# First routing of a mixture-of-experts kernel: the slots of the first two pairs of tiles ahead of their dense expert work

## What is computed

```python
x = x + 0.5 * ffn(layernorm(x), ...)
x = x + attention(layernorm(x), ...)
x = x + 0.5 * ffn(layernorm(x), ...)

def ffn(x, ...):
    scores = sigmoid(x @ gate_weight.T)              # 32 experts in 8 groups
    sfc = scores + bias
    # the 4 groups with the largest maximum, in them the 6 largest experts
    # combine weights: scores of the six, normalized, times 2.5
    for each expert: acc += c[:, None] * (silu(x @ gate.T) * (x @ up.T) @ down.T)
    shared = (silu(x @ shared_gate.T) * (x @ shared_up.T)) @ shared_down.T
    return acc + shared
```

## Time and profile before

| | us |
|---|---|
| median of three runs | 1548.52 |
| lowest and highest of the three | 1545.78 and 1552.76 |
| the profiled execution | 1545.28 |
| its span in the profile | 1543.5 |
| PE busy in the span | 1330.7 |
| POOL busy in the span | 924.0 |
| DVE busy in the span | 1067.6 |

### The profile page before, as it was taken

The page is one execution under the profiler, slowest core; times in us unless marked ns, Lnnn a source line. Parts: engine busy times, 40 slices in busy tenths (PEclk is TensorE's granted clock), DMA queues, the critical chain, the costliest instruction groups (busy, mean ns, idle before and its releaser), DMA issues. The chain is left out here.

```text
span 1543.5 us, 49298 instructions
## 1 busy us (share of the span) xinstructions
PE 1330.7 (86%) x9680; PEld 1132.0 (73%) x9681; DVE 1067.6 (69%) x5488; ACT 649.9 (42%) x2311; POOL 924.0 (60%) x981
## 2 busy tenths in 40 slices
PE   6867652899999999899999899844999999999896
PEld 5756541688888888678767677624888888888885
DVE  5676654577777777567568888872777777777585
ACT  3333330455555555300466666712555555555110
POOL 2777777466655666532027776774666666666687
PEclk9777885899999999999989999956999999999998
DMA  9963333555555555298013333433555555554799
GB/s 309 401 238 128 127 128 128 152 179 176 174 177 177 173 176 178 86 331 293 2 49 136 133 133 135 143 142 125 177 181 172 179 173 178 168 176 136 237 309 325
DMA packets 156143, 275.47 MB, mean 178 GB/s; under 512 B 29094, under 2 KB 108475, under 8 KB 156096
## 3 DMA queue, kind: packets, MB, share of 16 engines
q1 hardware_dynamic: 112000, 157.39, 33.0%
q0 software_dynamic: 39936, 113.33, 20.2%
q10 hardware_dynamic: 4160, 4.19, 0.8%
HBM read 147.90 MB, written 135.27 MB: 183 GB/s over the span
## 5 line engine op out<-in xcount | busy, mean ns | idle before, releaser
L633 POOL DMA_INDIRECT answers<-yb,didx x448 | 440.2, 983 | 316.5 <-issue 197.0
L672 PE MATMUL ps<-wgu,xbt 128*128 x1792 | 463.7, 382 | 0.0
L672 PEld LDWEIGHTS ps<-wgu,xbt 128*128 128x128 f32 x1792 | 307.4, 192 | 23.4
L1623 DVE SCALAR_TENSOR_TENSOR hb<-ps,wcol,sg 128x128 f32<-128x128 f32 x448 | 157.2, 351 | 168.3 <-ACT sg L1214 106.5
L617 POOL DMA_INDIRECT dispatch_rows<-blk,idx x192 | 189.5, 987 | 137.0 <-issue 124.0
L672 PE MATMUL ps<-wdn,hbt 128*128 x896 | 267.2, 380 | 1.8 <-ACT hbt L1218 1.8
L589 POOL DMA_INDIRECT dispatch_rows<-blk,idx x192 | 187.3, 975 | 81.8 <-issue 80.6
L1611 DVE SCALAR_TENSOR_TENSOR picked<-iota_e,etab,blk 128x32 f32<-128x32 f32 x896 | 190.3, 250 | 64.3 <-DMA blk<-dispatch_rows 34.8
L1214 ACT ACTIVATE sg<-ps 128x128 f32<-128x128 f32 x448 | 124.2, 277 | 234.8 <-PE ps L672 234.8
L773 PE MATMUL ps<-ident,blk 128*128 128x128 f32 x896 | 172.8, 275 | 37.2 <-DMA blk<-dispatch_rows 37.2
L1208 ACT COPY xbt<-ps 128x256 f32<-128x256 f32 x448 | 168.0, 375 | 70.4 <-PE ps L773 70.1
(11 more groups left out here) (217 smaller groups left out, 2016.3 us busy)
## 6 DMA issues: line engine op xcount, KB each, us to landing
blk<-dispatch_rows SPq DMA_DIRECT2D x448, 160.0 KB
ans<-answers SPq DMA_DIRECT2D x54, 512.0 KB, 4.5
ans<-answers SPq DMA_DIRECT2D x54, 256.0 KB, 4.4
wgu<-in_gate_up SPq DMA_DIRECT2D x32, 256.0 KB
answers<-yb,didx POOLq DMA_INDIRECT x448
dispatch_rows<-blk,idx POOLq DMA_INDIRECT x384, 2.5
dispatch_rows<-padt SPq DMA_DIRECT2D x32, 160.0 KB
yb<-answers SPq DMA_DIRECT2D x10, 512.0 KB, 5.0
```

Source lines behind the costliest of these rows:

```text
L633: pool.indirect_dma_start(out=answers_dram, out_offset=bass.IndirectOffsetOnAxis(ap=didx[:, q:q + 1], axis=0), in_=yb[:, q, :], in_offset= ...
L672: return nc.tensor.matmul(out_, lhs, rhs, start=start, stop=stop)
L1623: v.scalar_tensor_tensor(out=hb[:, j, :], in0=ps[:, GU + j, I:2 * I], scalar=wcol[:, q:q + 1], in1=sg[:, j, :], op0=ALU.mult, op1=ALU.mult ...
```

## The change

For pair 0 the order on three engines is another: the slots come before the dense expert work that stood between. The first statistics are taken for two tiles and then for two more, in place of four at once; tile 1's transposition goes into another bank of PSUM, so both tiles are transposed before either's logits. On VectorE pair 0's step also takes the statistics of tiles 4 to 7, pair 2's norms and the whole choice and slots of pair 1; pair 1's step is left with its dense work. The fifth scatter of pair 0 no longer waits for norms.

```diff
             def pair(p, q0):
                 for m in range(2 * TOPK):
-                    if m == 4 and pair_exists(p + 2):
+                    if m == 4 and pair_exists(p + 2) and not (isinstance(p, int) and p == 0):
                         pool.wait_ge(s.xn, p * 2 + 6)
...
         def pe_route(pe, s):
             def body(p, k):
+                if isinstance(p, int) and p == 0:
+                    pe_route_rk(pe, s, p, VO)
+                    pe_shared_gu(pe, s, 1, 1)
+                    transposed(1, 1 - k)
+                    for t in range(2):
+                        pe_shared_dn(pe, s, t, t)
+                    gate_up(1)
+                    pe.wait_ge(s.rkr, 1)
+                    pe_route_rk(pe, s, 1, VO)
+                    return
                 transposed(p + 1, 1 - k)
-                positive(pe, s.rkr, p)
-                pe_route_rk(pe, s, p, VO)
+                if not (isinstance(p, int) and p == 1):
+                    pe.wait_ge(s.rkr, p)
+                    pe_route_rk(pe, s, p, VO)
                 for t in range(2):
                     pe_shared_dn(pe, s, p * 2 + t, t)
                 gate_up(p + 1)
-            transposed(0, 0)
+            pe_route_t(pe, s, 0, 0)
+            pe_route_t(pe, s, 1, 1, FIRST_RT)
+            pe_route_lg(pe, s, 0, 0)
+            pe_route_lg(pe, s, 1, 1)
             pe.wait_ge(ld_shared, N_SHARED)
-            gate_up(0)
+            pe_shared_gu(pe, s, 0, 0)
...
         def act_route(act, s):
             def body(p, k):
+                if isinstance(p, int) and p == 0:
+                    act_route_rows(act, s, p, k)
+                    shared(p)
+                    transposed(p + 1, 1 - k)
...
         def v_route(v, st, s):
             def body(p, k):
+                if isinstance(p, int) and p == 0:
+                    v_norm(v, s, 1, 1, 2)
+                    v_route_groups(v, st, s, 0)
+                    v_route_six(v, st, s, 0)
+                    v_route_weights(v, st, s, 0, 0)
+                    v_route_ranks(v, st, s, 0, VO)
+                    v_route_slots(v, st, s, 0, 0)
+                    hidden(0)
+                    v.wait_ge(ld_x[1], 16)
+                    statistics(2)
+                    v_norm(v, s, 2, 0, 0)
+                    v_route_groups(v, st, s, 1)
+                    v_route_six(v, st, s, 1)
+                    v_route_weights(v, st, s, 1, 1)
+                    v_route_ranks(v, st, s, 1, VO)
+                    v_route_slots(v, st, s, 1, 1)
+                    add_shared(0)
+                    return
+                if isinstance(p, int) and p == 1:
+                    hidden(1)
+                    add_shared(1)
+                    v.wait_ge(ld_x[2], 16)
+                    return
...
             v.wait_ge(ld_x[0], 16)
-            statistics(0)
+            v_statistics(v, st, 0, 2)
             v_norm(v, s, 0, 0, 0)
+            v_statistics(v, st, 2, 2, at=2)
```

More of the change, by code:

```diff
@@ L591, in pair @@
                         in_=rows[:, q, :], in_offset=None).then_inc(s.scat[q], 16)
[L592 to L596, removed]
+            pairs_by_two(pool, lambda p, k: pair(p, 2 * k), NT // 2)
         def pool_route_paced(pool, s):
@@ L672, in mm, with pe_route_t @@
             return nc.tensor.matmul(out_, lhs, rhs, start=start, stop=stop)
-        def pe_route_t(pe, s, i, q):
+        def pe_route_t(pe, s, i, q, bank=RT):
             pe.wait_ge(s.xn, i + 1)
-            positive(pe, s.xts, i)
+            if bank == RT:
+                positive(pe, s.xts, i)
             for c in range(KC):
-                m = pe.transpose(ps[:, RT, c * P:(c + 1) * P], xn[:, q, c * P:(c + 1) * P], ident[:])
+                m = pe.transpose(ps[:, bank, c * P:(c + 1) * P], xn[:, q, c * P:(c + 1) * P], ident[:])
             m.then_inc(s.xt, 1)
@@ L701, in build @@
         SHARED_GU, SHARED_DN = 0, 2
+        FIRST_RT = SHARED_DN + 1
         def pe_shared_gu(pe, s, i, j):
@@ L1154, in pe_pass_b, with act_route_xt @@
             pairs_by_two(pe, body, NT // 2 + 2)
-        def act_route_xt(act, s, i, q):
+        def act_route_xt(act, s, i, q, bank=RT):
             j = q % 2
@@ L1166, in act_route_xt @@
                 positive(act, s.store[j], visits(i, j, 2, 16))
-            act.copy(xnt[:, j, :], ps[:, RT, 0:D]).then_inc(s.xts, 1)
+            act.copy(xnt[:, j, :], ps[:, bank, 0:D]).then_inc(s.xts, 1)
         def act_route_ex(act, s, p):
@@ L1197, in body @@
             def body(p, k):
[L1198 to L1201, removed]
+                if isinstance(p, int) and p == 0:
+                    act_route_rows(act, s, p, k)
+                    shared(p)
+                    transposed(p + 1, 1 - k)
+                else:
+                    shared(p)
+                    transposed(p + 1, 1 - k)
+                    act_route_rows(act, s, p, k)
+            act_route_xt(act, s, 0, 0)
+            act_route_xt(act, s, 1, 1, FIRST_RT)
+            act_route_ex(act, s, 0)
             pairs_by_two(act, body, NT // 2)
@@ L1392, in mean_of, with v_statistics @@
             return mv[:, bass.ds(i, 1), 0:1].rearrange("p a b -> p (a b)")
-        def v_statistics(v, st, i, n, steps=3):
+        def v_statistics(v, st, i, n, steps=3, at=0):
             st.sync()
@@ L1398, in v_statistics @@
             for t in range(n):
-                st.did(v.bn_stats(stats4[:, t, :], xtile(i + t)))
+                st.did(v.bn_stats(stats4[:, at + t, :], xtile(i + t)))
             st.sync()
@@ L1402, in v_statistics @@
             for t in range(n):
-                st.did(v.bn_aggr(mv4[:, t, :], stats4[:, t, :]))
+                st.did(v.bn_aggr(mv4[:, at + t, :], stats4[:, at + t, :]))
             st.sync()
-            inverse_root(st, mv4[:, 0:n, 1], rstd4[:, 0:n], newt[:, 0, 0:n], newt[:, 1, 0:n],
-                         steps)
+            which = slice(at, at + n)
+            inverse_root(st, mv4[:, which, 1], rstd4[:, which], newt[:, 0, which], newt[:, 1, which], steps)
         def v_norm(v, s, p, k, at):
@@ L1544, in body @@
                 add_shared(p)
-                if isinstance(p, int) and p < 2:
-                    v.wait_ge(ld_x[p + 1], 16)
                 if k == 0:
```

## The result

| | us |
|---|---|
| before, median of 20 runs | 1553.85 |
| after, median of 20 runs | 1548.78 (1539.31 to 1554.35) |
| ratio | 0.9971, 95% interval 0.9957 to 0.9984 |
| the profiled execution after, and its span | 1552.99, 1551.2 |

The ratio is a gain of 4.5 us, with an interval from 2.5 to 6.7 (0.0029, 0.0016 and 0.0043 of 1553.85). The forecast was 4.2 us. The level is another matter: before stands 5.3 us above the median of its first three runs (1548.52), and after 4.5 above the forecast that started from it.

The account below looks back on a forecast made before the run. GpSimd's scatter queue was taken to bound the first routing: 5.8 us gained at its start, 1.6 lost at pair 1, so 4.2 off the 1548.52 median gives 1544.3 us; the forecast's own range 1541 to 1547, overall 1539 to 1551.

Parts of the forecast that it names:

- Bound and path: First routing: GpSimd's scatter queue ends last, so moving its start moves the program's end by as much while it stays fed.
- First scatter: Head of GpSimd's queue, pair 0: slots done at 19.7, first scatter at 20.7 in place of 26.51, 5.8 us earlier.
- by twos: VectorE's first statistics for two tiles, then two more: 0.85 us off before the first norm, root chain paid again.
- the bound of 2.4 us: VectorE's root chains: if time were proportional to columns, pair 0's choice would start 2.4 us earlier; not in the forecast.
- Ranks ahead of the dense work: TensorE, pair 0: rank product directly behind `sel` at 17.0, before tile 1's gate and up, removing the 5.0 us stall.
- What is late next: Pair 1 feeding the queue: ninth scatter waits for `sel` until 32.95, thirteenth at 38.15; 1.6 us lost, 4.2 us kept.
- row copy done at 37.0, allowing 38.0: ScalarE's row copy of pair 1 ends at 37.0, allowing a scatter at 38.0, before the thirteenth's 38.15.
- table switch: Rival, ScalarE before pair 1's row copy: one more 1.3 us drain, thirteenth scatter 39.3, gain 3.0, 1545.5 us; chance 0.03.
- Full gain: Rival: TensorE's clock fast from 18, nothing delays the thirteenth scatter at 36.3; gain 6.0, 1542.5 us; chance 0.16.
- late clock: Rival: TensorE's clock rises only at about 31, in pair 1's gate and up; gain 2.2, 1546.3 us; chance 0.25.
- stages behind 275 change in length: Sign that the forecast is wrong: program stages after the first routing, behind about 275 us, change in length.
- How the numbers follow: Whole-program timing: about 0.5% (7.7 us) can be told from no change; faster by more 0.11, slower 0.03, within 0.86.

Follow-up runs that it names:

- e6: Kernel before the change, with the first scatter also waiting for `sel` of pair 1; timed ratio 1.0063, interval 1.0036 to 1.0089.
- e10: Changed kernel with both tiles' gate and up before the ranks, pair 1's row copy earlier, its norms behind pair 0's slots; ratio 0.9963 to the kernel before.
- e4: Changed kernel with statistics of the first four tiles at once again; rerun after a slow series: first scatter 20.60, last 268.03 us.
- e9: Changed kernel with both tiles' gate and up ahead of pair 0's rank product; rerun after a slow series: first scatter 20.87, last 266.19 us.
- e2: Changed kernel with ScalarE's row copy of pair 1 moved to the end of pair 0's step; thirteenth scatter 38.00, last 0.7 us earlier.
- e7: Changed kernel with statistics of tiles 4 to 7 ahead of pair 0's hidden product; rerun after a slow series: last scatter 265.28 us, not timed over many runs.
- e1: Changed kernel, pair 0's ninth scatter no longer waiting for `sel` of pair 1; thirteenth scatter 39.20, last 268.01 us.
- e3: Changed kernel without the ninth scatter's wait for `sel` and with pair 1's row copy earlier; ratio 0.9977, interval 0.9954 to 0.9999.

## Why the prediction was right or wrong

*Bound and path: right.* The queue carries its shift to the end (e6: 9.0 later in the queue, 9.8 in time; e10: 5.8 earlier in the queue, 5.7 in time).

*First scatter: right within 0.3.* 20.94 for 20.7. 0.13 are the load of x, which released the statistics at 4.58 where the earlier trace rows have 4.45. The first norms ended at 8.87 for 8.68. That by twos is a gain was wrong (e4): the 0.9 us off the start of the choice came from both transposes standing ahead of the logits (12.79 with the statistics by fours), and the second chain of roots, which the prediction did price in full, takes a bit of it back (12.99). The chain took 2.38 us for 2 columns as it had for 4 (5.76 to 8.14), so the bound of 2.4 us was none. With that the rows agree with what the Trainium skill says of a fixed cost in each instruction (VectorE: DVE Perf Modes, "The TRN2 errata — SBUF-src ops pay a fixed extra latency per instruction").

*Ranks ahead of the dense work: the order was right, the reading of it wrong.* The 5.0 us between `sel` and the ranks were called the stall to be had, and the ranks ahead of all of it the way to have it. Of the 5.0 us the dense piece took 1.6 (to 19.45, `sel` at 17.86), and the transposes and logits of pair 1 most of the rest. In e9 the 32 records still stand ahead of the ranks; they begin 1.9 us earlier than before (11.45, 13.35 in the earlier trace rows), end at 17.10, and `sel` is done at the same moment, so the first scatter is as early. Transposing both tiles first had already taken the dense piece off the path; moving the ranks ahead of its second half only delayed that half, and with it pair 1.

*What is late next: the waits are the ones named, but one was put at nothing.* The ninth scatter was forecast at 32.95, with a wait for `sel`, and is at 32.91. For the thirteenth the step that failed is "row copy done at 37.0, allowing 38.0": the sum has no wait for the row copy. The copy ended at 37.77 and the thirteenth scatter waited 0.59 for it, so it is at 38.58 and not at 38.15; e2, with the copy moved, has it at 38.00 without a wait. The 37.0 took the clock as fast from 22 on. It did rise where the forecast had it (the transposes at 22.07 took 0.64 for two records, those at 23.65 took 0.42), but it fell again during pair 2's transposes. Behind the thirteenth another 0.5 went, which I had not counted: 229.4 us to the last scatter where the kernel before took 228.9. The experiments without a wait there took 228.8 to 229.5, so this is the spread of single executions. So the queue gave 3.3 us where the sum said 4.2, and that the timed 4.5 lies so near 4.2 is partly luck.

*The rivals.* The table switch of the Trainium skill (ScalarE: Activation LUTs, "What ACT_TABLE_LOAD costs") didn't show: load at 35.75 for 1.28, `ex` at 37.04, no drain between. Full gain was the result of e7, by another order. The late clock (chance 0.25) did occur, in e1 and e4: the down product ended at 29.68 and 29.46 and the thirteenth scatter started at 39.20 and 39.03, where the rival had 29.8 and 40.1. The instructions of e1 on TensorE are those of the changed kernel, which presumably meets either clock; its profiled execution had the early one, and how often each occurs in the 20 runs is not known. The sign "stages behind 275 change in length" came true for one stretch (164.4 to 172.8), with the reservation made above.

*How the numbers follow: here the prediction failed.* The step is "About 0.5% (7.7 us) is what a measurement of this kernel can tell from no change", taken from the spread of three runs. What the runs showed in its place: with 20 runs of each kernel the interval is 0.13% to each side, and a gain of 0.29% is clear of it. The forecast gain was near the measured one, and calling it no change was the mistake. The level was off too: the measured 1548.78 lies 1.8 us above the forecast's own range of 1541 to 1547. 1544.3 is the forecast gain taken from the median of three runs, 1548.52, where 20 runs give 1553.85; 4.2 below that would be 1549.7.

## What to carry to other kernels

When the start of a saturated queue is moved forward, follow the next items that must be there: the gain is what the slowest of them allows, and waits that stand one behind the other have to be tried together, since removing one may show nothing (e1) or a part (0.7 us, e2). Look first for a wait of the feeding engine on work that nobody needs yet; moving one line behind two others (e7) added 2.7 us in the trace to the 3.3 that the reordering of three engines had kept. Compare small gains by the times at which the shared queue starts and ends, not by the span of one execution; look whether TensorE's clock rose at the same place in both, since that alone moved the thirteenth scatter by 0.6 us; and take the resolution of a measurement from its number of runs.

## What the runs showed of the hardware that was not expected

In the first 30 us the clock column stood at 1.00 (12 to 14 us in the windows above, and 28 to 30 in e1), while 16 dense records took 3.76 in the changed kernel, the down product took 3.76 in e1 at 25.92, and 32 dense records took 6.10 or 5.65 (e9); at full level 32 take 3.73 and the down product 1.97. The durations, not the column, tell the level at the start of a program.

The same instructions of TensorE met a clock that rose at different times. In the changed kernel, e2, e3 and e7 it rose at about 23 us. In e1, whose TensorE code and times up to there are the same (within 0.15 us), it rose at about 30, between the down product (3.76) and the end of the gate and up behind it (32 records in 4.29). What decides between the two was not tried.

In one series of runs all kernels took 16 to 17% longer. In e7_hidden_late of that series ScalarE had stood for 11.89 us by 38.27 and VectorE for 3.54 by 38.51, with a releaser that the profile calls remote, at a time at which the expert weights are loaded. What held them was not tried.
